# Whole-array products in place of column-tile pairs, and four PSUM banks for the first and the last feed-forward

## The reference

```python
x = x + 0.5 * ffn(layernorm(x))
x = x + attention(layernorm(x))
x = x + 0.5 * ffn(layernorm(x))

def ffn(x):                       # w_gate, w_up: 352 x 128, w_down: 128 x 352
    gate, y = fp4_linear(x, w_gate), fp4_linear(x, w_up)
    return fp4_linear(silu(gate) * y, w_down)   # fp4_linear rounds x and w to an FP4 grid by blocks of 16
def attention(x):                 # 16 heads of 64
    q, k, v = split_heads(x @ w_q), split_heads(x @ w_k), split_heads(x @ w_v)
    p = softmax(q @ k.T / 8)      # 512 x 512 for each head
    y = merge_heads(p @ v) @ w_proj + b_proj + x
    return layernorm(y) * gamma + beta
```

## Time and profile before

| | |
|---|---|
| median of three executions | 2347.0 us |
| the profiled execution | 2348.62 us, span 2346.8 us from first to last instruction |
| TensorE busy | 2217.9 us (95%), 14537 matmul records |
| VectorE, GpSimd, ScalarE busy | 1670.9, 1470.6, 1194.5 us |
| mean granted TensorE clock | 0.980 |
| one image in the steady part | 137.0 or 137.6 us, TensorE busy 135.84 or 136.24 |

### The profile page before, as it was taken

How to read it: one execution, slowest core, us unless ns; L and a number is a source line. 1 busy time by engine, 2 the same in 40 slices (tenths; PEclk the granted TensorE clock), 3 DMA queues, 4 the chain that set the end, 5 groups by cost and what they waited for, 6 DMA issues and landing times.

```text
span 2346.8 us, 38775 instructions
## 1 busy us (share of the span) xinstructions
PE 2217.9 (95%) x14537; PEld 1120.2 (48%) x14537; DVE 1670.9 (71%) x2734; ACT 1194.5 (51%) x1813; POOL 1470.6 (63%) x1419
## 2 busy tenths in 40 slices
PE   3799999999999999999999999999999999999983
PEld 1344445545454554545555454555545454454541
DVE  4465778777787777778777777877777787776643
ACT  1345554545555465555546555554555555454531
POOL 2266666766676675667667576766757676575642
PEclk9799999999999999999999999999999999999985
DMA  1000000000000000000000000000000000000000
GB/s 53 5 7 2 2 7 2 11 2 11 2 7 7 2 11 2 11 2 7 6 2 11 2 11 2 7 7 2 11 2 11 2 6 6 2 7 2 7 2 9
DMA packets 167495, 15.85 MB, mean 7 GB/s; under 512 B 148304, under 2 KB 166928, under 8 KB 167312
## 3 DMA queue, kind: packets, MB, share of 16 engines
q1 hardware_dynamic: 167312, 13.39, 4.9%
HBM read 7.03 MB, written 4.19 MB: 5 GB/s over the span
## 4 chain that ended last, share of the span: by engine, by line
PE 82%; DVE 12%; issue 4%; POOL 1%; ACT 1%; DMA 0%; SPq 0%; POOLq 0%
PE pS L920 21%; PE pO L947 18%; PE pM L904 9%; PE pX L932 6%; PE pX L968 5%; PE pM L1066 5%; DVE nmax L769 3%; PE pM L957 3%; PE FpF L248 2%; PE LpF L283 2%; PE FpF L283 2%; PE LpF L259 2%; PE LpF L248 2%; PE FpF L259 2%; DVE ON L863 1%
## 5 line engine op out<-in xcount | busy, mean ns | idle before, releaser
L634 POOL TENSOR_TENSOR ES<-ES,E 128x512 f32<-128x512 f32 x512 | 701.2, 1390 | 212.6 <-ACT E L721 210.2
L721 ACT ACTIVATE E<-pS 128x1024 f32<-128x1024 f32 x512 | 522.9, 1021 | 411.9 <-PE pS L920 407.6
L769 DVE TENSOR_REDUCE nmax<-pX 128x2 fp32r<-128x1024 f32 x512 | 621.9, 1215 | 129.3 <-PE pX L932 126.4
L947 PE MATMUL pO<-E,VA 128*64 128x512 f32 x2048 | 552.3, 618 | 0.0
L628 POOL TENSOR_TENSOR ES<-E 128x512 f32<-128x512 f32 x256 | 321.4, 1276 | 260.9 <-ACT E L721 260.6
L904 PE MATMUL pM<-xf,w_raw 128*64 128x512 f32 x1024 | 266.1, 598 | 3.1 <-DVE QL L872 2.4
L932 PE MATMUL pX<-KH,QH 64*128 64x512 f32 x1024 | 249.5, 426 | 7.7 <-DVE nmax L769 5.0
L920 PE MATMUL pS<-QH,KH 64*128 64x512 f32 x1024 | 255.5, 496 | 0.0
L920 PEld LDWEIGHTS pS<-QH,KH 64*128 64x128 f32 x1024 | 95.4, 183 | 253.3 <-issue 252.0
L932 PEld LDWEIGHTS pX<-KH,QH 64*128 64x128 f32 x1024 | 189.7, 306 | 51.3 <-DVE nmax L769 12.4
L920 PE MATMUL pS<-SH,onesr 64*128 64x512 f32 x1024 | 203.3, 393 | 0.0
(11 more groups left out here) (135 smaller groups left out, 3291.2 us busy)
## 6 DMA issues: line engine op xcount, KB each, us to landing
RROW<-RC SPq DMA_DIRECT2D x512, 2.0 KB, 2.0
xin<-in_L_attn_x SPq DMA_DIRECT2D x16, 256.0 KB, 3.0
SH<-nmax SPq DMA_DIRECT2D x256, 2.0 KB, 2.0
LC<-LROW SPq DMA_DIRECT2D x256, 2.0 KB, 2.1
out<-X SPq DMA_DIRECT2D x16, 256.0 KB, 2.5
w_raw<-in_L_attn_w_q SPq DMA_DIRECT2D x1, 512.0 KB, 4.7
w_raw<-in_L_attn_w_k SPq DMA_DIRECT2D x1, 512.0 KB, 5.5
w_raw<-in_L_attn_w_v SPq DMA_DIRECT2D x1, 512.0 KB, 6.7
```

Source lines behind the costliest of these rows:

```text
L634: ins = g.tensor_tensor(ES[par][:, hd, :], ES[par][:, hd, :], E[s][:, hd, :], ALU.add)
L721: a.activation(E[s][:, :, :], pS[:, :, :], ACT.Exp).then_inc(s_exp, 1)
L769: v.tensor_reduce(nmax[px % 2][:, :, t:t + 1], pX[:, :, :], AX.X, ALU.max, negate=True).then_inc(s_max, 1)
L947: ins = pe_.matmul(pO[half(hd), :], VA[of][:, kt, j * 128 + 64 * hd:j * 128 + 64 * hd + 64], E[kt][:, hd, :], start=kt == 0, stop=kt == KT ...
```

## The change

Four things change.

1. Q, K, V, gate, up, down and projection become one matmul of 128 stationary columns where they were two of 64. `times_v` and `row_sums` keep their column halves.
2. `F.spare` and `L.spare` name four banks (own bank, pO, pM, one of pS). The first feed-forward of image 0 and the last one of image 15 put the products of the four row blocks in these four banks: a gate product waits for nothing, an up product for the silu of its own block only.
3. At the start the weights are quantised in `L.h`, and the normalisation and quantisation of the first x are written ahead of and between the steps of the weights on each engine. The loop starts at b = -1. The first V products move one or two steps later (`rounds_at`).
4. For the last image the gamma product and the sum X2 run on VectorE, not on GpSimd.

```diff
+    def apart(self, c):
+        return c == self.alone
+    def bank(self, c, k):
+        return self.spare[k] if self.apart(c) else self.pF
...
-        for n in range(2):
-            ins = self.nc.tensor.matmul(self.pF[half(n), 0:FF], self.xqT[:, k * 128 + 64 * n:k * 128 + 64 * n + 64],
-                                        self.wguT[:, 0, 0:FF], start=True, stop=True)
-        ins.then_inc(self.s_gate, 1)
+        self.nc.tensor.matmul(self.bank(c, k)[:, 0:FF], self.xqT[:, k * 128:k * 128 + 128],
+                              self.wguT[:, 0, 0:FF], start=True, stop=True).then_inc(self.s_gate, 1)
...
-        if k == 0:
+        if self.apart(c):
+            pe.wait_ge(self.s_silu, 4 * c + k + 1)
+        elif k == 0:
             pe.wait_ge(self.s_silu, 4 * c + 4)
...
-        for b in range(-2, B + 2):
+        for b in range(-1, B + 2):
...
+        if s == 2:
+            return {-1: (0,), 0: (2,)}.get(i, ())
+        if s == 3:
+            return (1,) if i == -1 else (i + 3,) if 0 <= i < ROUNDS - 3 else ()
...
+        F.spare, F.alone = (F.pF, pO, pM, pS[:, 0, :]), 0
+        L.spare, L.alone = (L.pF, pO, pM, pS[:, 0, :]), B - 1
...
+                norm_x.scales(nc, pool, neg_half, 0)
+                L.qh.divide(nc, pool, 0, L.h[:, 0:NW], slice(0, NW // BLK))
+                F.pool_divide_x(pool, 0)
+                L.qh.rescale(nc, pool, 0, L.h[:, 0:NW], slice(0, NW // BLK))
+                F.pool_rescale_x(pool, 0)
...
-                    for hd in range(2):
-                        ins = pe_.matmul(pM[half(hd), :], w_raw[:, k, p * 128 + 64 * hd:p * 128 + 64 * hd + 64], x,
-                                         start=True, stop=True)
-                    return ins
+                    return pe_.matmul(pM[:, :], w_raw[:, k, p * 128:p * 128 + 128], x, start=True, stop=True)
```

More of the change, by code:

```diff
@@ L257, in pe_up @@
             pe.wait_ge(self.s_h, 4 * c + k)
[L258 to L261, removed]
+        self.nc.tensor.matmul(self.bank(c, k)[:, 0:FF], self.xqT[:, k * 128:k * 128 + 128],
+                              self.wguT[:, 1, 0:FF], start=True, stop=True).then_inc(self.s_up, 1)
     def pe_h(self, pe, c, k):
@@ L281, in pe_down @@
             for ch in range(FT):
[L282 to L285, removed]
+                ins = self.nc.tensor.matmul(self.pF[:, t * D:(t + 1) * D], self.hqT[:, ch, t * 128:t * 128 + 128],
+                                            self.wdT[:, ch, :], start=ch == 0, stop=ch == FT - 1)
         ins.then_inc(self.s_down, 1)
@@ L842, in last_ffn @@
                             norm_y.moments(nc, dve, c, Yacc[1 - bpar])
+                        if t == 15 and c == B - 1:
+                            dve.wait_ge(norm_y.s_out, c + 1)
+                            v.tensor_tensor(tiles(L.xm[:, :]), tiles(L.xm[:, :]), each_tile(gamma), ALU.mult).then_inc(s_gam, 1)
+                            dve.wait_ge(s_gam, c + 1)
+                            dve.wait_ge(s_x1b, c + 1)
+                            wait(dve, s_out, 16 * c)
+                            v.tensor_tensor(X2[:, :], L.xm[:, :], X1[1 - bpar][:, :], ALU.add).then_inc(s_x2, 1)
                         if t == 15:
@@ L963, in project @@
                     pe.wait_ge(s_norm, i - 2)
-                    pe.wait_ge(s_max, 4 * min(i + 2, NP) if isinstance(i, int) else 4 * (i + 2))
+                    pe.wait_ge(s_max, 4 * min(i + 2, NP))
                     wait(pe, s_yacc, i - 3)
                     for t in range(T):
[L967 to L970, removed]
+                        ins = pe_.matmul(pX[:, 0, t * 128:(t + 1) * 128], ON[:, t * 128:t * 128 + 128], wp[:, po, :],
+                                         start=True, stop=True)
                     ins.then_inc(s_proj, 1)
@@ L979, in first_ffn @@
                             F.pe_x(pe, c)
+                        if t == 1 and c == 0:
+                            pe.wait_ge(s_wT, 3)
                         if 1 <= t < 5:
@@ L1039, in body @@
                                 pe.wait_ge(s_xf, b + 2)
-                            if isinstance(i, int) and i == -2:
+                            if i == -2:
                                 pe.wait_ge(s_raw, 48)
                                 pe.wait_ge(s_wp, 16)
-                            wait(pe, s_va, i + 3 if not isinstance(i, int) else min(i + 3, ROUNDS) if i >= 0 else (0, 2)[i + 2])
+                                pe.wait_ge(s_ones, 4)
+                                pe.wait_ge(s_one, 1)
+                            wait(pe, s_va, min(i + 3, ROUNDS) if i > 0 else 2 if i == 0 else 0)
                             per_head(0, p2, x).then_inc(s_q, 1)
@@ L1053, in body @@
                             project(i, p)
[L1054 to L1068, removed]
+                        for r in rounds_at(i, s):
+                            kt, of, xb = round_place(i, p, bpar, r)
+                            pe.wait_ge(s_klo, min(i + 3, NP))
+                            wait(pe, s_va, r)
+                            if there(i - 2, NP):
+                                pe.wait_ge(s_norm, i - 1)
+                            elif there(i - 1, NP):
+                                pe.wait_ge(s_lrow, i)
+                            if p == 5:
+                                pe.wait_ge(s_xf, b + 2)
+                            pe_.matmul(pM[:, :], xf[xb][:, kt * 128:kt * 128 + 128], w_raw[:, 2, of * S:of * S + S],
+                                       start=True, stop=True).then_inc(s_v, 1)
                 steps(pe, body)
```

67 lines of the change are left out of this document (32 added, 35 removed).

## The result

Five executions of the changed kernel gave 2357.55 to 2360.0 us, median 2358.2; five of the kernel before beside them had the median 2347.89. The ratio is 1.0045, with a 95% interval of 1.0031 to 1.006: slower, by 10 us. The forecast was 2362, range 2334 to 2394. The profiled execution took 2358.06 us, with a span of 2356.3.

A forecast was written before the change was run, and what follows sets the result against it. The prediction took TensorE, busy 95% of the span, as the bound. Its sum was 2348.6 + 51 - 9 - 17.5 - 9.5 = 2363.6 us; the median of runs lies 1.6 lower, so 2362, range 2334 to 2394.

The forecast's parts named there:

- The layout term, +51: TensorE in the 16 images: layout changes go from 82 to 94 an image, costing +3.2 us each, +51 in all.
- Rival 1: Entry into the whole array: as short as the transposes', 0.05 us, so +29 for the images and 2340 us; chance 0.22.
- Rival 2: Behind pO: column halves to whole array is free, images show no difference, ends' -27 stand alone, 2320 us; chance 0.08.
- Rival 3: In the images: transposes and whole-array products drain each other too, +38 us, so 2400 us; chance 0.14.
- Rival 4: Images and ends: added drains hide in waits, full 18 us back, or clock rises early, 2350 us; chance 0.08.
- The short parts, 0 in the sum: Down and projection: 112 parts an image keep 0.11 us each, taken as 0; uncovered loads would cost 90 us.
- The give-back, -9: TensorE's waits in the images shrink as its stages lengthen: between 0 and 18 us back, half taken, -9.
- The start, -17.5: Before the images: earlier first gate -7.5, eight products in four banks -8, V products moved -2; sum -17.5 us.
- First gate: At the start: with x ahead of the weights, the first gate product starts near 22 us, not 29.50: -7.5.
- Eight products to the last h: First feed-forward at the start: with four banks the products follow each other, 10.5 us for 18.4: -8.
- The end, -9.5: Last feed-forward and gamma: eight products in four banks -8, gamma and sum on VectorE -1.5; sum -9.5 us.
- another 1 to 2 us: Feed-forward products in four banks: further gain if uninterrupted products bring the clock up, not in the sum.

The follow-up runs named there:

- e7: e2 with the V products alone as whole-array matmuls; 2330.9 us, ratio 0.9928 to the kernel before.
- e3: e2 with products whole-array from a transpose to the stage's end, the others in halves; 2308.32 us, ratio 0.9838 to the kernel before.
- e4: Changed kernel with the projection alone written again as column halves, the other six kinds whole; 2371.14 us, ratio 1.0105 to the kernel before.
- e2: Changed kernel with all seven kinds of product back in column halves, new ends and four banks kept; 2317.13 us, ratio 0.988 to the kernel before.
- e1: Kernel before with the whole-array products alone, its start, end and single bank kept; 2393.71 us, ratio 1.0203 to the kernel before.
- e6: e2 without the four banks at the ends, one bank per feed-forward again; 2336.0 us, ratio 0.9954 to the kernel before.

## Why the prediction was right

**The layout term, +51, stands.** The count of 82 and 94 changes is what the order has. Priced as in the table, an image has 13.7 us of it before and 16.8 now (17.10 without the 0.27 of the short parts; both with the 32 entries into the column halves), +3.1 for the 3.2 that I took. The disputed number was e, the entry into the whole array: 1206.89 - 1205.92 is 0.97, so e is 0.10. Rival 1 took 0.05 and falls. That this entry is the first weight load, laid bare, is my reading and not shown: it goes by the columns for the untransposed kinds (0.051 for 64, 0.104 for 128), but no run separates the load from what else a change brings. (The pair that the prediction calls "the gate pair before transposes", L259 in the earlier trace rows, is an up pair; the reading is the same.) The Trainium skill's rule, in "TensorE: Matmul & The Clock Gate", section "LDWEIGHTS (loading the stationary operand)", would have the load at 128 / 1.2 = 107 ns, as an estimate from that page; if the entry is the load, the trace agrees for this one (0.104) and not for the transposing one (0.056).

**Rival 2 falls** by pO to Q, 1.01 and not 0.91, and by e7, where up ahead of the whole V takes the same 0.10 more. The Trainium skill's rule in "TensorEngine Tiling (Array Packing)", section "Key Properties", that a change of mode drains the array, holds for this pair too. **Rival 3 falls** by up to transposes, 0.59, and by e3, which is built on the two sharing a layout and gains 11 us in the attention. **Rival 4** had its condition fulfilled, and its time didn't come: more than its 18 us was given back and the clock rose early at both ends, but the layout's +50 stood, and the short parts and the first and last images, at 0 in the sum, took some 9 of it back.

**The short parts, 0 in the sum, cost a little:** 0.112 for 0.109. With 112 parts that is 0.27 us an image, 4 us in all. Not the 90 that an uncovered load would have cost, and e4 shows that they are not the place to look.

**The give-back, -9, was mis-sized.** I took half of TensorE's idle time, 1.16 us an image. But the ends of matmuls are modelled, and a modelled end covers a short wait. This place of the changed kernel has no idle time in the trace:

```profile
1196.83 1.08 PE L963 MATMUL pO<-E,VA 128*64 128x512 f32 x4
1197.89 0.86 PE L255 MATMUL FpF<-wguT,FxqT 128*128 128x352 f32 x2
```

Yet the gate starts 1.06 behind pO, where other stages have 1.01. Summed over an image by starts the waits are 4.0 us before and 2.85 after. They gave back 1.2 us an image, 19 us, which is more than the 18 that I had put as the most. Layout +50, short parts +4 and waits -19 make +35 to +36, and the measured periods differ by 2.25 us, 36 in sixteen images; the attention as a whole grew by 40.6. The 4 to 5 us between lie in the first and last images, where the stages are filled otherwise. From the first E to the load of x at 286.00 (297.75 before), some one and a half images, the changed kernel takes 7.7 us more, where 2.25 an image would be 3.3. A part of that is the clock, which is granted at half for a while there:

```profile
125.90:129.31 3.41, 3.41 (x14) 1.61 (x14) 1.06 (x1) 2.29 (x3) 3.33 (x5) 0.50 0.01 2
```

What TensorE did in these 3.41 us would take some 1.7 at the full clock (an estimate from the granted share). Shortly before, its V product had waited 1.94 us for ON of VectorE. The kernel before and e2 have waits of this length too (up to 1.9 and 2.0 us) and no such fall; e1, e4 and e6 have the fall. So it doesn't follow the form of the products, and why it came stays open, as does the rest of the 4 to 5 us.

**The start, -17.5, came out at -19.45.** First gate -7.7 (I said -7.5). The way there was a little other than I had it: the transposes of x start at 20.00, beside the last weight copy (20.25 to 20.74), not behind it. Eight products to the last h -9.0 (-8). From there to the down product 12.1 us before and after, as expected. Down to Q -0.5. Q to the first E, where the V products moved out, -2.3 (-2). e6 against e2 gives the bank's part as 12.8, more than -9.0: in e2 the eight products ran faster still, see below. The V products' part in the -2.3 was not measured alone.

**The end, -9.5, came out at -11.7.** The eight products brought 9.8 where I had 8, because the clock rose during them: the first took 1.34, the fifth 0.59 (differences of the starts in the rows above), and the granted clock of the stretch from 2327.98 to 2336.40 is 0.83, after 0.50 before the change. The prediction had left that out of the sum as "another 1 to 2 us". Gamma now takes 0.69.

So the mechanism and the sign were right. That the total for the attention came within 1.4 us is in part luck, since errors of opposite sign met in it. The profiled execution came out 5.5 us under the sum (2358.06 for 2363.6): the ends -4.2, the attention -1.4, and this last is, roughly, waits -10 and layout -1 against short parts +4 and the +5 of the first and last images.

## What to carry to other kernels

Count the changes of array layout along TensorE's order before changing the shape of a product: here 12 more changes on top of 82 in an image, with a dearer entry for 28 of them, cost 41 us of 2159, while halving the products' instructions brought nothing. Give each product the layout of its neighbours: whole behind transposes, halves behind halves (e3 gained 11 us in the attention by that alone). And read waits of TensorE from differences of starts, since modelled ends hide the short ones: of 4.0 us in an image before the change the idle time shows 1.16.

## What the runs showed that I had not expected

The speed of the first products differs between kernels that do the same up to there. In e2 the first gate product starts at 21.65 and the eight follow each other at 0.59 from the first on:

```profile
21.65 0.81 PE L104 MATMUL FpF<-wguT,FxqT 128*64 128x352 f32 x4 [0.78 <-ACT FxqT L317]
22.26 0.79 PE L104 MATMUL pO<-wguT,FxqT 128*64 128x352 f32 x4
...
25.81 0.79 PE L104 MATMUL pS<-wguT,FxqT 128*64 128x352 f32 x4
```

In the changed kernel the first took 1.31, and the next three 1.17 each up to the start of the fifth at 26.67. In e6 their records last 1.44 each, to the last of the eight, with a wait between:

```profile
22.57 1.44 PE L104 MATMUL FpF<-wguT,FxqT 128*64 128x352 f32 x4 [0.78 <-ACT FxqT L317]
25.12 1.44 PE L104 MATMUL FpF<-wguT,FxqT 128*64 128x352 f32 x4 [1.11 <-DVE Fh L343]
```

Four passes of 352 columns in 1.17 us are 1.2 GHz, in 0.59 us 2.4 GHz. Yet the changed kernel's first stretch shows a granted clock of 1.00 (third column from the end):

```profile
21.84:26.67 4.83, 4.83 (x8) 2.84 (x9) 1.48 (x3) 1.39 (x3) 0.00 (x0) 1.00 0.00 0
```

This 1.00 is no measurement. The clock's record in a trace begins with its first change, and the views count the time ahead of it as full clock. The first entry, a rise, stands at 26.91 us in the changed kernel, at 20.91 in e2, at 57.80 in e6 and at 65.25 in the kernel before. That fits the products: in the changed kernel they are fast from the fifth on (it starts at 26.67), in e2 all eight are, in e6 and in the kernel before none is. Ahead of the first entry the clock is therefore read from the products, here 1.2 GHz, and not from the third column from the end; the mean clock of 0.980 counts that time as full as well.

The early rise is why the start of e2 is 2.8 us shorter than that of the changed kernel: the last of its eight products starts 2.76 us earlier, at 25.81 against 28.57. In e3 the first entry stands at 26.28, and its start is 2.3 us longer than e2's. That e6 has no rise there is also a part of what it loses. Why the rise came 6 us earlier in e2 stays open: each kernel has one profile, and up to the first gate e2 and the changed kernel have the same products, 0.2 us apart. Differences of 2 to 3 us between the starts of these kernels carry no conclusion here.

Besides, the entry into transposes costs 0.056 us where that into plain products of 128 float32 columns, in row halves or on the whole array, costs 0.104, although transposes and whole-array products are one layout.
